# Attention keys projected once: the half-swap of the sine product moves from TensorE to a DMA in SBUF, and keys and values share two banks in turn

## What is computed

```
lat = layer_norm(latents); ctx = layer_norm(context)
q = lat @ Wq;  k, v = split(ctx @ Wkv)           # 16 heads x 64
k = concat([k1*cos - k2*sin, k2*cos + k1*sin])   # k1, k2: the two halves (32 wide) of each head
attn = softmax(clip((q @ k.T) / 8, -11, 11));  out = (attn @ v) @ Wo + bo
```

## Time and profile before

| | us |
|---|---|
| median of 3 runs | 390.94 |
| lowest and highest | 389.09, 391.6 |
| the profiled execution | 388.52 |
| its span, first to last instruction | 386.4 |
| PE busy in the span | 321.9 |
| DVE busy | 269.6 |
| POOL busy | 217.0 |
| ACT busy | 155.5 |

### The profile page before, as it was taken

How to read it: one execution, slowest core, us unless ns; L and a number is a source line. 1 busy time by engine, 2 the same in 40 slices (tenths; PEclk the granted TensorE clock), 3 DMA queues, 4 the chain that set the end, 5 groups by cost and what they waited for, 6 DMA issues and landing times.

```text
span 386.4 us, 6595 instructions
## 1 busy us (share of the span) xinstructions
PE 321.9 (83%) x2566; PEld 215.9 (56%) x2566; DVE 269.6 (70%) x459; ACT 155.5 (40%) x282; POOL 217.0 (56%) x200
## 2 busy tenths in 40 slices
PE   6699999999999989789999999599998986630444
PEld 6476666667776656457766566377665545310131
DVE  4886426337754799777585999774549879599844
ACT  3464544555324546215345556343444540100500
POOL 4767344355544483929346677973445876546070
PEclk9999999999999999969999999999999999755656
DMA  8730000000000000000000000000000000000000
GB/s 248 181 53 2 27 2 1 2 2 3 0 2 2 1 2 0 3 0 2 2 0 2 1 2 2 1 15 2 1 2 0 2 3 14 0 0 0 0 0 27
DMA packets 10157, 5.82 MB, mean 15 GB/s; under 512 B 2768, under 2 KB 9744, under 8 KB 10128
## 3 DMA queue, kind: packets, MB, share of 16 engines
q1 hardware_dynamic: 9072, 5.29, 5.3%
q10 hardware_dynamic: 1056, 0.13, 0.2%
HBM read 4.89 MB, written 0.52 MB: 14 GB/s over the span
## 4 chain that ended last, share of the span: by engine, by line
PE 53%; DVE 23%; POOL 10%; issue 6%; ACT 5%; DMA 2%; SPq 1%; DVEq 0%; POOLq 0%; ACTq 0%
PE sc L493 11%; PE pv L507 11%; PE sums L523 5%; POOL prod L823 5%; PE pj_k L434 5%; DVE prod L815 4%; PE pj_k L436 4%; PE pj_k L435 4%; DVE att L1003 4%; ACT e L688 3%; DVE o L1020 3%; PE side L580 3%; DMA prod<-in_L_xattn_Wq_dram 2%; DVE prod L823 2%; POOL wvS L1212 1%
## 5 line engine op out<-in xcount | busy, mean ns | idle before, releaser
L688 ACT ACTIVATE e<-sc 128x1024 f32<-128x1024 f32 x64 | 65.7, 1026 | 100.9 <-PE sc L493 100.9
L1225 POOL TENSOR_SCALAR e<-e 128x1024 f32<-128x1024 f32 x64 | 71.6, 1119 | 34.7 <-ACT e L688 30.9
L1218 POOL TENSOR_TENSOR krot<-kcos,ksin 128x512 f32<-128x512 f32 x32 | 41.7, 1304 | 69.7 <-DVE ksin L903 69.7
L493 PE MATMUL sc<-qs,ks 64*128 64x256 f32 x768 | 62.5, 295 | 6.3 <-ACT e L688 5.7
L493 PEld LDWEIGHTS sc<-qs,ks 64*128 64x128 f32 x768 | 49.4, 185 | 28.5 <-issue 16.6
L507 PE MATMUL pv<-e,v 128*64 128x256 f32 x512 | 64.0, 393 | 0.0
L507 PEld LDWEIGHTS pv<-e,v 128*64 128x64 f32 x512 | 34.5, 139 | 24.2 <-issue 9.3
L903 DVE TENSOR_TENSOR kcos<-pj_k,cosT 128x512 f32<-128x512 f32 x32 | 22.0, 688 | 30.2 <-PE pj_k L436 29.8
L523 PE MATMUL sums<-e,sum_rows 128*32 128x256 f32 x512 | 30.9, 382 | 5.3 <-POOL e L1225 5.3
L840 DVE TENSOR_TENSOR ks<-krot,ks 128x512 fp32r<-128x512 f32 x32 | 34.0, 1063 | 0.0
L823 POOL TENSOR_TENSOR prod<-att,kv 128x1024 f32<-128x1024 f32 x8 | 27.7, 3474 | 8.9 <-ACT att L779 8.6
(11 more groups left out here) (215 smaller groups left out, 596.3 us busy)
## 6 DMA issues: line engine op xcount, KB each, us to landing
ctx_in<-in_ctx_dram SPq DMA_DIRECT2D x4, 256.0 KB, 5.0
prod<-in_L_xattn_Wkv_dram SPq DMA_DIRECT2D x2, 512.0 KB, 6.0
x_in<-in_x_dram SPq DMA_DIRECT2D x1, 512.0 KB, 5.8
prod<-in_L_xattn_Wq_dram SPq DMA_DIRECT2D x1, 512.0 KB, 6.6
wo<-in_L_xattn_Wo_dram SPq DMA_DIRECT2D x1, 512.0 KB, 8.4
fwe<-in_L_ffn_We_dram SPq DMA_DIRECT2D x1, 512.0 KB, 4.3
out_dram<-x_in SPq DMA_DIRECT2D x4, 128.0 KB, 1.8
fbup_r<-in_L_ffn_bup_dram SPq DMA_DIRECT2D x1, 128.0 KB, 6.5
```

The costliest lines, as they stand in the source:

```text
L493: last = nc.tensor.matmul(sc[:, h, c * NT:(c + 1) * NT], ks[rows, j % 3, k_part, chunk], qs[rows, j % 2, q_part, :], start=(k_part + q_par ...
L688: nc.scalar.activation(e[:, j % 3, :, 2 * half:2 * half + 2, :].rearrange("p h c n -> p h (c n)"), sc[:, :, :], ACT.Exp, scale=SCALE).then ...
L1218: nc.gpsimd.tensor_tensor(krot[:, j % 2, :], kcos[:, j % 2, :], ksin[:, j % 2, :], ALU.add)\
L1225: nc.gpsimd.tensor_scalar(a, a, EXP_HIGH, EXP_LOW, ALU.min, ALU.max).then_inc(s_clip, 1)
```

## The change

Keys are projected once. `keys(j)` makes the three `wkA` matmuls alone, into one bank; `wkB`, with its four copies on DVE at the start, is gone. DVE multiplies that one bank by the sines first (`ksin`) and by the cosines second (`kcos`). The sine product's half rows are exchanged afterwards: SP waits for `ksin(j)` and issues four DMAs of 32 rows by 512 floats (64 KB each) from `ksin` to a new tile `kswap`. The signs of the sine table are turned round, because the exchange now comes after the product. POOL adds `kcos + kswap`, waits for the DMAs of that pair, and does so behind `clip(s,0)`, no longer ahead of it. Keys and values take the banks `pj_k0` and `pj_k1` in turn, in program order, each waiting for what the projection two before it left there.

```
 PE   keys(j):
-        split3(pj_k[0], wkA[:, 0, cols], wkA[:, 1, cols], ctxT[:, 0, :], ctxT[:, 1, :])
-        split3(pj_k[1], wkB[:, 0, cols], wkB[:, 1, cols], ctxT[:, 0, :], ctxT[:, 1, :])
+        bank_free("keys", j)
+        split3(key_bank(j), wkA[:, 0, cols], wkA[:, 1, cols], ctxT[:, 0, :], ctxT[:, 1, :])
 DVE  key_products(j):
-        for i, (dst, bank, trig) in enumerate(((kcos, pj_k[0], cosT), (ksin, pj_k[1], sinT))):
-            dve.wait_ge(s_kproj, 2 * j + i + 1)
+        dve.wait_ge(s_kproj, j + 1)
+        for dst, trig in ((ksin, sinT), (kcos, cosT)):
 SP   after load_ctx(1):
+            def swap_halves(j):
+                sp.wait_ge(s_kmul, 2 * j + 1)
+                if j >= 2:
+                    sp.wait_ge(s_krot, j - 1)
+                for r in range(4):
+                    to, at = HALF * r, HALF * (r ^ 1)
+                    sp.dma_start(kswap[to:to + HALF, j % 2, :], ksin[at:at + HALF, j % 2, :]).then_inc(s_kswap[j % 2], 16)
+            for j in range(2):
+                swap_halves(j)
             sp.dma_start(wo[:, :, :], Wo.rearrange("(g p) n -> p g n", p=128)).then_inc(ld["wo"], 16)
...
-            for b in range(2, NB):
-                load_ctx(b)
+            load_ctx(2)
+            for j in range(2, NPAIR):
+                if j == PAIRS:
+                    load_ctx(3)
+                swap_halves(j)
 POOL rotate(j):
                 pool.wait_ge(s_kmul, 2 * j + 2)
+                pool.wait_ge(s_kswap[j % 2], 64 * (j // 2 + 1))
-                nc.gpsimd.tensor_tensor(krot[:, j % 2, :], kcos[:, j % 2, :], ksin[:, j % 2, :], ALU.add)
+                nc.gpsimd.tensor_tensor(krot[:, j % 2, :], kcos[:, j % 2, :], kswap[:, j % 2, :], ALU.add)
 POOL, the loop over slots:
-                if slot + KV_AHEAD < NPAIR:
-                    rotate(slot + KV_AHEAD)
                 second_layer(slot, -1)
                 if 0 <= slot < NPAIR:
                     clip(slot, 0)
+                if slot + KV_AHEAD < NPAIR:
+                    rotate(slot + KV_AHEAD)
```

More of the change, by code:

```diff
@@ L174, in value_units, with value_units_at_first, projections @@
     return []
-def value_units_before(slot):
-    return sum(len(value_units(s)) for s in range(-KV_AHEAD, slot))
+def value_units_at_first(n):
+    return n < 4
+def projections():
+    units = []
+    for slot in range(-KV_AHEAD, LAST_SLOT):
+        if slot + KV_AHEAD < NPAIR:
+            units.append(("keys", slot + KV_AHEAD))
+        for n in value_units(slot):
+            if not value_units_at_first(n):
+                units.append(("values", n))
+    return units
+PROJECTIONS = projections()
+PLACE = {unit: i for i, unit in enumerate(PROJECTIONS)}
 def xattn_ffn(nc, x, ctx, cos, sin, ln_lat_g, ln_lat_b, ln_ctx_g, ln_ctx_b, Wq, Wkv, Wo, bo,
@@ L323, in xattn_ffn @@
         s_kmul = sem("s_kmul")
+        s_kswap = [sem(f"s_kswap{i}") for i in range(2)]
         s_krot = sem("s_krot")
@@ L384, in value_bank, with key_bank @@
         def value_bank(n):
-            return first_value_banks[n] if n < len(first_value_banks) else pj_k[n % 2]
+            return first_value_banks[n] if value_units_at_first(n) else pj_k[PLACE["values", n] % 2]
+        def key_bank(j):
+            return pj_k[PLACE["keys", j] % 2]
         @block.sync
@@ L436, in split3, with bank_free @@
                 return nc.tensor.matmul(out_ap, w_lo, m_hi, start=False, stop=True)
+            def bank_free(kind, n):
+                if PLACE[kind, n] < 2:
+                    return
+                kind, n = PROJECTIONS[PLACE[kind, n] - 2]
+                if kind == "keys":
+                    pe.wait_ge(s_kmul, 2 * n + 2)
+                else:
+                    pe.wait_ge(s_v, n + 1)
             def keys(j):
@@ L444, in keys @@
                     pe.wait_ge(s_wk, 1)
[L445 to L453, removed]
+                bank_free("keys", j)
+                split3(key_bank(j)[:, :], wkA[:, 0, cols], wkA[:, 1, cols], ctxT[:, 0, :], ctxT[:, 1, :]).then_inc(s_kproj, 1)
             def queries(j):
@@ L470, in values @@
                     pe.wait_ge(s_wv, 1)
-                if n >= len(first_value_banks):
-                    pe.wait_ge(s_v, n - 1)
-                    pe.wait_ge(s_kmul, 2 * min(slot + KV_AHEAD + 1, NPAIR))
+                if not value_units_at_first(n):
+                    bank_free("values", n)
                 rows = slice(128 * c, 128 * c + 128)
@@ L639, in _ @@
                 for n in value_units(slot):
-                    values(n, slot)
+                    values(n)
                 side_at(slot, "b")
@@ L1117, in _ @@
             tokens_normalise(0)
[L1118 to L1124, removed]
             dve.wait_ge(s_wqhi, 1)
```

13 lines of the change are left out of this document (7 added, 6 removed).

## The result

| | before | changed kernel |
|---|---|---|
| median of 4 runs, same chip | 391.27 | 405.31 |
| ratio, with its 95% interval | | 1.0373 (1.033 to 1.0415) |
| profiled execution, its span | 388.52, 386.4 | 406.07, 404.0 |
| mean granted clock of PE in it | 0.93 | 0.887 |

One of the four runs of the changed kernel was disturbed (434.79) and is left out of the ratio; the median takes it in, and is 404.55 without it. The prediction was 393.3, range 386 to 398.5; the time lies 6.8 us above the range. "Slower by over 1%" had 0.33.

What follows compares the result with a forecast made beforehand. PE was taken as the bound, except in two stretches paced by DVE and POOL. Start +9.1, clock +2.8, stretches +2.2, slot 29 +1.6, matmuls -13.3 sum to +2.4 us: median 390.94 becomes 393.3, range 386 to 398.5.

Steps and rivals of the forecast that it cites:

- Slower by over 1%: Whole kernel: the outcome of a time over 394.9 us, given a chance of 0.33.
- PE's gain of 13.3 us in 19 slots: Slots 2 to 12, 17 to 20 and 25 to 28, bound by PE: three matmuls fewer gain 0.70 us each.
- 3.24 us from the end of `ksin` to `rotate`: Each exchange: the fourth issue starts 1.44 us after `ksin`, plus 1.8 to land; upper bound 4.34.
- the 4.5 that was named as a sign of being wrong: Each exchange: over 4.5 us, or under 2.5, from the end of `ksin` would show the prediction wrong.
- In a slot bound by PE this is hidden: Slots bound by PE: the exchange's 3.24 us costs nothing, since rotated keys are needed a slot later.
- The start, +11.9: Start: exchange 2 behind SP's loads delays slot 1's exponentials by 9.1 us; PE's lower clock adds 2.8.
- The price of the clock: Start, behind PE's stall: work at about half clock adds 2.8 us.
- So each of the two stretches gets 1.1 us longer: 127.5 to 166 and 209 to 249 us, paced by DVE and POOL: later `rotate` delays POOL's product; 2.2 us together.
- Slot 29, +1.6: Last slot with keys: `rotate` 2.6 us later delays ACT's expert copies and PE's sums; 1.6 taken between 0.9 and 2.6.
- The exchange lands late: Rival: landings of 2.9 us cost 3.3 us more in both DVE/POOL stretches and slot 29; 396.6 us, chance 0.25.
- The loads drain faster: Rival, start: without backlog pair 2 lands at 32.7, losing 6.0 us instead of 9.1; 390.2 us, chance 0.20.
- the start does not stall: Rival, start: exchange 2 not held by earlier loads, about 1 us lost; 382.4 us, chance 0.10.

Runs made afterwards that it cites:

- eight issues: Changed kernel with the start's loads spread behind later exchanges, each exchange's four transfers issued in two halves, against the kernel before: 425.06 us, ratio 1.0891.
- two queues: Changed kernel with the start's loads spread behind later exchanges, two of each exchange's four transfers issued by POOL, against the kernel before: 389.66 us, ratio 0.9969.

## Why the prediction was wrong, step by step

The span grew by 17.6 us and not by 2.4. Of the 15.2 us missed, 6.0 lie in slots 21 to 24, 2.4 in the start, 2.2 from slot 29 on, 1.9 in slots 2 to 12, 1.4 in 25 to 28 and 1.3 in 13 to 16. The step that failed most is the price of the two stretches of DVE and POOL: 2.2 us predicted for both, 9.4 measured.

- **PE's gain of 13.3 us in 19 slots: right.** Without exchange and with the old order these slots gave 12.9. With the exchange, slots 2 to 12 kept 5.8 of 7.7; of the 1.9 lost, 1.4 belong to exchanges, of which six took 4.0 us and five 4.7 to 5.8. Slots 25 to 28 kept 1.4 of 2.8: there the rotate's new place costs 1.3 without any exchange (38.2 for 36.8).
- **"3.24 us from the end of `ksin` to `rotate`": mis-sized.** It was 4.0 in most pairs, inside the bound of 4.34, and over the 4.5 that was named as a sign of being wrong in some. The issue of a 64 KB transfer in SBUF took 0.59, not the 0.43 of a load, and a landing 2.0, not 1.8. The Trainium skill's estimate of 2.15 ("DMA: Bandwidth & Descriptors", "Anatomy of one DMA") was a little nearer to the 2.0. That section describes DMAs issued by GpSimd, and the change's are issued by SP; with two queues both kinds landed in 2.0.
- **"In a slot bound by PE this is hidden": right**, with far less room than it sounded; eight issues showed the edge.
- **The start, +11.9: right in mechanism, 2.4 short.** The order of SP's queue was read correctly, and `ctx_in` went out at 30.36 for 29.0. But it took 8.0 us to land, not 6.8, and exchange 2 landed 0.8 us behind it (one of its issues lasted 1.87 us): it was rotated at 39.23, while 35.8 was taken for its landing. So the exponentials came 12.4 us later, not 9.1. The price of the clock erred the other way, 1.9 us for 2.8, and that the total came as near as 2.4 is in part luck; PE's clock had also fallen before the stall, and not by it. It was the largest single loss, and the loads' place in the queue was its cause: moving them gave 11.0 of the 14.3 back.
- **"So each of the two stretches gets 1.1 us longer": wrong.** They got 2.4 and 7.1. I followed one chain, rotate to POOL's product to DVE's last reduction, in one slot (15). Not followed were the second clip behind the rotate in slot 13 (PE waited 4.44 us with its sums, 1.51 before), ACT's expert copies behind the high copy in slot 21 (4.75, 0.20 before), and the half clock after each of them. Nor did I give the rotate's new place a price of its own, though it moves POOL's long products against DVE's; without any exchange it costs 4.4 us in slots 21 to 24. In the changed kernel this overlap does not occur, and the 7.1 us come from the other waits and the half clock behind them.
- **Slot 29, +1.6: right place, mis-sized.** The wait of PE for ACT's copies behind `key_hi` was named, and I took a middle between 0.9 and 2.6. It was 3.8: PE waited 4.50 us there instead of 0.47, and the matmuls behind the wait ran at half clock (2.03 us for 1.13), for which the term had nothing.
- **The rivals.** "The exchange lands late" was the nearest in sign, but its mechanism (a landing over 2.3 us in each exchange) was not what happened: the median was 2.0, and only behind the loads of the start did it reach 5.1 to 6.3. "The loads drain faster" and "the start does not stall" fell.

What stays open: why some issues of the same transfer took up to 2.04 us instead of 0.59; why slots 21 to 24 keep half of the order's cost when the overlap is gone; and when PE's clock falls behind a wait (of the waits of 2.93 us at 166.11 and at 248.69 and of 2.94 us above, the second was followed by full clock, the other two by half).

## What to carry to other kernels

A DMA between two compute steps has to be priced with everything that stands behind its waiter on each in-order engine: here POOL's clip (slot 13) and ACT's expert copies (slots 21 and 29) turned 4 us of latency into PE's idle time. Put a latency-bound transfer ahead of bulk loads on its queue, and its consumer where nothing waits behind it. Moving an instruction on GpSimd is not free for adding no work (here it cost 1.2%): look at which of VectorE's two-input operations it will then meet.

## What the runs showed of the hardware

- A DMA of 32 rows by 2 KB from SBUF to SBUF occupied SP for 0.59 us (0.51 to 2.04) and landed 2.0 us after its issue (5.1 to 6.3 behind thirteen loads and a context of 256 KB); in eight parts of half the size the landing was 1.8. GpSimd issued it in 0.54 us, with the same landing.
- VectorE's two-input operations in SBUF and GpSimd's take turns instruction by instruction: 1.95 us became 4.63 and 0.68 became 3.00 on VectorE, 1.04 became 2.65 and 2.9 became 4.47 on GpSimd.
- PE at the lower clock cost 1.7 us at a time (3.64 for 1.93, 3.68 for 1.95), behind the waits of 4.4 to 6 us for which the rows behind them are given here, and behind some of 2.9.
